# Keys loaded and turned before queries, and beta's product with the queries moved to TensorE, in the opening stage of a fused attention and mixture-of-experts kernel

## What is computed

```python
xn = layernorm(x)
# s: attention on xn
x_norm = layernorm(xn) * gamma + beta
q, k, v = x_norm @ qkv[:, :512], x_norm @ qkv[:, 512:1024], x_norm @ qkv[:, 1024:]
attn = softmax(causal(q @ k.T / sqrt(512)))
s = (attn @ v) @ o_proj + xn
# f: mixture of 8 experts (top 2 by the router) plus a shared expert
f = routed(xn, router_w, wg, wu, wd) + shared(xn, sg, su, sd)
out = x + s * silu(f)
```

## Time and profile before

| | |
|---|---|
| median of 3 runs | 1148.88 us (1148.87 to 1150.69) |
| profiled execution | 1149.01 us, of which 1147.2 us is the span of the trace |
| TensorE busy | 1130.9 us, 99% of the span |
| VectorE busy | 571.8 us, 50% |
| ScalarE busy | 473.0 us, 41% |
| granted TensorE clock, mean | 0.998 |

### The profile page before, as it was taken

One profiled execution on the slowest core, in us unless ns is written; L12 is line 12 of the kernel. 1 busy time (PEld: TensorE's weight loads), 2 busy tenths in 40 slices (PEclk: granted clock), 3 DMA queues, 4 the chain that ended last, 5 costly groups with the idle time before them and its releaser, 6 DMA issues. The chain is left out here.

```text
span 1147.2 us, 21220 instructions
## 1 busy us (share of the span) xinstructions
PE 1130.9 (99%) x6598; PEld 625.7 (55%) x6599; DVE 571.8 (50%) x1236; ACT 473.0 (41%) x859; POOL 420.3 (37%) x656
## 2 busy tenths in 40 slices
PE   8999999999999999999999999999999999999997
PEld 5555555555556555555555555554444444444443
DVE  7876667667469221221112211122477377367467
ACT  5544444344332223332223322234654545545643
POOL 1333233332400222222222222213755754764763
PEclk9999999999999999999999999999999999999999
DMA  9899999988533698998997877766876777766364
GB/s 283 241 227 214 229 245 222 226 206 243 127 78 74 126 202 198 204 204 203 206 193 189 179 182 179 181 163 155 166 183 172 166 160 189 157 160 183 107 161 116
DMA packets 365003, 209.31 MB, mean 182 GB/s; under 512 B 304308, under 2 KB 314816, under 8 KB 364936
## 3 DMA queue, kind: packets, MB, share of 16 engines
q1 hardware_dynamic: 354104, 172.76, 64.3%
q0 software_dynamic: 10800, 35.69, 12.1%
q10 hardware_dynamic: 32, 0.02, 0.0%
HBM read 89.44 MB, written 46.01 MB: 118 GB/s over the span
## 5 line engine op out<-in xcount | busy, mean ns | idle before, releaser
L706 PE MATMUL pair<-arena 128*128 (+2 forms) x3240 | 506.2, 313 | 0.3 <-issue 0.2
L706 PEld LDWEIGHTS pair<-arena 128*128 128x128 f16 x3240 | 315.7, 98 | 183.2 <-issue 1.5
L1646 DVE SCALAR_TENSOR_TENSOR arena<-pair,slot_unit,arena 128x352 f32<-128x352 f32 x71 | 41.4, 584 | 269.5 <-ACT arena L1536 269.5
L713 PE MATMUL bank<-arena 128*128 x639 | 149.4, 379 | 0.0
L1536 ACT ACTIVATE arena<-pair,slot_unit 128x352 f32<-128x352 f32 x71 | 39.3, 553 | 205.5 <-PE pair L706 202.4
L1251 POOL COPY arena<-token_of 128x1 uint32 (+1 forms) x71 | 12.9, 182 | 264.1 <-issue 107.0
L1942 PE MATMUL pair<-arena 128*128 128x512 f16 (+3 forms) x576 | 98.4, 326 | 1.1 <-ACT arena L2010 0.6
L713 PEld LDWEIGHTS bank<-arena 128*128 128x128 f16 x639 | 62.5, 98 | 66.3
L1955 PE MATMUL bank<-arena 128*128 128x512 f16 x411 | 93.6, 379 | 0.3 <-DVE arena L2122 0.3
L1253 POOL DMA_INDIRECT arena<-xn_rows,arena x71 | 71.4, 1006 | 55.6 <-POOL arena L1251 52.5
L1922 PE MATMUL bank<-arena 128*128 128x512 f16 x384 | 86.1, 379 | 0.0
(11 more groups left out here) (205 smaller groups left out, 1354.4 us busy)
## 6 DMA issues: line engine op xcount, KB each, us to landing
slot_rows<-arena SPq DMA_DIRECT2D x71, 256.0 KB
arena<-in_L_attn_x_dram SPq DMA_DIRECT2D x64, 256.0 KB, 3.4
xn_rows<-arena SPq DMA_DIRECT2D x32, 260.0 KB, 2.5
shared_rows<-arena SPq DMA_DIRECT2D x32, 256.0 KB, 3.4
arena<-shared_rows SPq DMA_DIRECT2D x32, 256.0 KB, 3.1
out_dram<-arena SPq DMA_DIRECT2D x31, 256.0 KB, 2.5
arena<-in_L_ffn_wg_dram SPq DMA_DIRECT2D x32, 176.0 KB, 3.0
arena<-in_L_ffn_wu_dram SPq DMA_DIRECT2D x32, 176.0 KB, 3.2
```

The costliest lines, as they stand in the source:

```text
L706: last = pe.matmul(bank[:, 0:width], xt[:, a, c, :], weights(c, b, col, width), start=(c == 0 and i == 0), stop=(c == KC - 1 and i == 2))
L713: last = pe.matmul(bank[:, :], ht[:, a, c, :], weights(c, b), start=(start and c == 0 and i == 0), stop=(stop and c == HC - 1 and i == 2))
L1646: v.scalar_tensor_tensor(sbuf[u], u_banks[u][:, 0:H], slot_unit[u][:, 1:2], sbuf[u], ALU.mult, ALU.mult).then_inc(slot_h_ready, 1)
```

## The change

The keys' two loads are issued ahead of the queries' four. The keys are turned first, into banks 0 to 3, with `turn_small` behind the second row block. The queries are then turned by row block: one bank takes the four transposes of one row block, so it holds all that one block of 128 output rows needs. Three query blocks are turned, then the first product is made (its 12 matmuls ordered by part instead of by chunk), then the fourth query block, then the other products. The products go to banks 0, 1, 2, 3, 6, 7, 4, 6. The order of high and low parts becomes keys, three query blocks, two value blocks, the fourth query block, two value blocks. `keep_small` and `split_small` come first on their engines. The load of repeated beta and the four `beta_row` are removed. Instead `query_beta`, behind the second product, makes 16 float32 matmuls of one column, and `split_ab` reads the result with one added instruction.

```diff
-            turns = [("turn", m, n) for m in range(2) for n in range(KC)]
+            k_turns = [("turn", 1, n) for n in range(KC)]
+            q_turns = [("turn", 0, k) for k in range(KC)]
+            v_parts = [("split_v", 2, k) for k in range(KC)]
             products = [("product", m, n) for m in range(2) for n in range(KC)]
-            on_pe = turns + products
+            on_pe = k_turns + q_turns[:3] + products[:1] + q_turns[3:] + products[1:]
+            first_groups = k_turns + q_turns[:3] + v_parts[:2] + q_turns[3:] + v_parts[2:]
+            groups = first_groups + products[:2] + [("split_o", 0, k) for k in range(KC)] + products[2:]
...
             def sync(sp):
                 q_rows = qkv.rearrange("(c p) n -> p c n", p=P)
-                for k in range(KC):
-                    sp.dma_start(w_qkv[:, k, 0:D], qkv[k * P:(k + 1) * P, 0:D]).then_inc(q_loaded[k], 16)
                 for i in range(2):
                     rows = slice(i * KC // 2, (i + 1) * KC // 2)
                     sp.dma_start(w_qkv[:, rows, D:2 * D], q_rows[:, rows, D:2 * D]).then_inc(k_loaded[i], 16)
+                for k in range(KC):
+                    sp.dma_start(w_qkv[:, k, 0:D], qkv[k * P:(k + 1) * P, 0:D]).then_inc(q_loaded[k], 16)
...
-                sp.dma_start(beta_rows, beta.partition_broadcast(P)).then_inc(beta_loaded, 16)
...
+                def turn_q(k):
+                    pe.wait_ge(q_loaded[k], 16)
+                    if k == KC - 1:
+                        pe.wait_ge(lo_done, made("turn", 0, 0))
+                    for n in range(KC):
+                        part = pe.transpose(banks[bank_of[("turn", 0, k)]][:, n * P:(n + 1) * P],
+                                            w_qkv[:, k, n * P:(n + 1) * P], ident)
+                    part.then_inc(group_done, 1)
...
+                def query_beta():
+                    pe.wait_ge(affine_kept, 4)
+                    for n in range(KC):
+                        for k in range(KC):
+                            last = pe.matmul(small[:, qb_at + n:qb_at + n + 1], w_qkv[:, k, n * P:(n + 1) * P],
+                                             affine[:, 1, k:k + 1], start=(k == 0), stop=(k == KC - 1))
+                    last.then_inc(ab_done, 1)
+
+                def first_product():
+                    bank = banks[bank_of[("product", 0, 0)]]
+                    for i, (a, b) in enumerate(PARTS):
+                        if i == 0:
+                            pe.wait_ge(hi_done, made("turn", 0, 0))
+                        else:
+                            pe.wait_ge(lo_done, made("turn", 1, KC - 1) if i == 1 else made("turn", 0, 0))
+                        for c in range(KC):
+                            if i == 0 and c == 0:
+                                pe.wait_ge(lo_done, made("turn", 1, 0))
+                            last = pe.matmul(bank[:, :], turned[:, 0, c, a, 0:P], turned[:, 1, c, b],
+                                             start=(c == 0 and i == 0), stop=(c == KC - 1 and i == 2))
+                    last.then_inc(group_done, 1)
...
-                for m in range(2):
-                    for k in range(KC):
-                        turn_row(m, k)
-                for n in range(KC):
+                for k in range(KC):
+                    turn_k(k)
+                    if k == 1:
+                        turn_small()
+                for k in range(3):
+                    turn_q(k)
+                first_product()
+                turn_q(KC - 1)
+                for n in range(1, KC):
                     product(0, n)
-                    if n == 0:
-                        turn_small()
+                    if n == 1:
+                        query_beta()
                 beta_products()
...
-                def beta_row(n):
-
-                    dve.wait_ge(beta_loaded, 16)
-                    wait(dve, ab_done, n)
-                    v.tensor_tensor_reduce(weighed, banks[n][:, :], beta_rows, S_AB, 0.0, ALU.mult, ALU.add,
-                                           accum_out=ab[:, 0, n:n + 1]).then_inc(ab_done, 1)
...
                 def split_ab():
-                    dve.wait_ge(ab_done, KC)
                     dve.wait_ge(uw_done, 1)
+                    dve.wait_ge(ab_done, 1)
+                    v.tensor_scalar(ab[:, 0, :], small[:, qb_at:qb_at + KC], S_AB, None, ALU.mult)
```

More of the change, by code:

```diff
@@ L356, in fold_programs @@
             bias_made = sem("bias_made")
-            turns = [("turn", m, n) for m in range(2) for n in range(KC)]
+            k_turns = [("turn", 1, n) for n in range(KC)]
+            q_turns = [("turn", 0, k) for k in range(KC)]
+            v_parts = [("split_v", 2, k) for k in range(KC)]
             products = [("product", m, n) for m in range(2) for n in range(KC)]
-            on_pe = turns + products
[L362 to L365, removed]
+            on_pe = k_turns + q_turns[:3] + products[:1] + q_turns[3:] + products[1:]
+            first_groups = k_turns + q_turns[:3] + v_parts[:2] + q_turns[3:] + v_parts[2:]
+            groups = first_groups + products[:2] + [("split_o", 0, k) for k in range(KC)] + products[2:]
+            bank_of = {**{g: n for n, g in enumerate(k_turns)}, **dict(zip(q_turns, (4, 6, 7, 4))),
+                       **dict(zip(products, (0, 1, 2, 3, 6, 7, 4, 6)))}
             def made(kind, m, n):
@@ L372, in group_target @@
                 kind, m, n = groups[g]
+                if kind == "turn" and m == 0:
+                    return turned[:, 0, :, :, n * P:(n + 1) * P].rearrange("p c s t -> p s c t"), S_QKVO
                 if kind == "turn":
-                    return turned[:, m, n], S_QKVO
+                    return turned[:, 1, n], S_QKVO
                 if kind == "split_v":
@@ L482, in product @@
                 def product(m, n):
-                    bank = banks[bank_of[on_pe.index(("product", m, n))]]
-                    q = m * KC + n
-                    if m == 1:
+                    bank = banks[bank_of[("product", m, n)]]
+                    if m == 0:
+                        pe.wait_ge(lo_done, made("turn", 0, n))
+                    else:
                         pe.wait_ge(v_moved[n // 2], 32)
-                    wait(pe, ab_done, rows_before[q])
-                    if q >= 5:
-                        pe.wait_ge(lo_done, made("product", 0, q - 5))
+                    if (m, n) == (1, KC - 1):
+                        pe.wait_ge(lo_done, made("product", 1, 0))
@@ L490, in product @@
                     for c in range(KC):
-                        if n == 0:
-                            pe.wait_ge(lo_done, made("turn", 1, c) if m == 0 else made("split_o", 0, c))
+                        if m == 1 and n == 0:
+                            pe.wait_ge(lo_done, made("split_o", 0, c))
                         for i, (a, b) in enumerate(PARTS):
@@ L543, in banks_free @@
             def banks_free(pe, b):
-                pe.wait_ge(lo_done, (made("product", 0, 3), made("product", 1, 0), made("product", 1, 3))[b])
-                if b < 2:
-                    pe.wait_ge(ab_done, b + 3)
+                pe.wait_ge(lo_done, (made("product", 0, 1), made("product", 0, 3), made("product", 1, 3))[b])
             def turn_bias(pe):
@@ L588, in keep_small @@
                                          ).then_inc(affine_kept, 1)
[L590 to L594, removed]
                 keep_small()
+                for g in first_groups:
+                    high(*g)
                 high("product", 0, 0)
@@ L661, in keep_bias @@
                                     ).then_inc(bias_made, 1)
[L663 to L669, removed]
+                split_small()
+                for g in first_groups:
+                    low(*g)
+                    if g == q_turns[2]:
+                        stats(dve, 0)
                 normalise(dve, 0)
                 low("product", 0, 0)
-                split_small()
-                beta_row(0)
-                beta_row(1)
                 low("product", 0, 1)
```

18 lines of the change are left out of this document (6 added, 12 removed).

## The result

The changed kernel is slower: 1154.88 us in the median of 9 executions (1150.72 to 1156.42) against 1149.19 (1147.76 to 1152.09), a ratio of 1.0043 with a 95% interval of 1.0032 to 1.0054, or 4.9 us. Two more measurements of the same file gave 1.0036 (1.0022 to 1.0049) and 1.0049 (1.0032 to 1.0066). The forecast was 1149.4 with a range up to 1152.2. The profiled execution of the changed kernel took 1156.42 us with a span of 1154.7, so it lies above its median, where that of before lay on it.

The account below looks back on a forecast made before the run. TensorE, busy 99% of the span, was taken as the bound: -1.33 - 0.10 - 0.40 + 0.47 + 3.1 = +1.8 us there, 1.3 absorbed by stalls, +0.5 at the end; 1149.4 us on the median, range 1147.8 to 1152.2.

Parts of the forecast that it names:

- First product at 10.8: Start of TensorE's first product in the fold, forecast at 10.8 us instead of 12.13: -1.33 us.
- rival of the late rate: TensorE's clock stays low through the first product: D = 4.6, the end +3.3 us, 1152.2; chance 0.10.
- Added products, 3.1 us: The 16 float32 matmuls of `query_beta` on TensorE, taken as three passes of 65 ns each: 3.1 us in all.
- Of TensorE's 1.8 us, 1.3 are absorbed by stalls: Up to the down product near 65 us, existing stalls take 1.3 us of the delay; +0.5 reaches the end.
- D: Delay of TensorE behind `query_beta`, forecast +1.8 us; from there up the end moves by about D - 1.3.
- the mark: Start of the shared expert's down product that waits for a DMA transpose: 64.96 us before, forecast 65.46.
- the copy at 46.69: ScalarE's copy in the chain to the stalled down product, forecast 0.5 us late, behind silu(1)'s work ending at 47.2.
- TensorE's few waits follow its own pace: After 65 us TensorE's waits were to move along with it.
- within 0.2%: Outcome that the end differs by less than 0.2% (2.3 us), which can't be told from none; chance 0.75.
- the case with 0.19: Outcome that the kernel is slower: long passes, late rate and rests; chance 0.19.
- the four passes: Rival: float32 products in `query_beta` take four passes, added 4.2 us, the end +1.6, 1150.5; chance 0.20.
- the gain: Rival: float32 matmuls of `query_beta` cost one pass (1.0 us), D = -0.3, the end -0.7, 1148.2; chance 0.12.

Follow-up runs that it names:

- after_warm: The changed kernel with 14 instead of 10 warm-up transposes and nothing else; ratio 1.0067 to the kernel before.
- new_order_ratio: The changed kernel without `query_beta`: the key side of `bias_folds` multiplies the finished fold by beta over gamma, in the same float16 matmuls; ratio 1.0005.
- after_beta_twice: The changed kernel with `query_beta` made twice in a row, 7.0 us of float32 products instead of 3.5; ratio 1.0113.
- before_filled: The kernel before with eight more idle transposes between the queries' and the keys' turns; ratio 1.0014.
- old_ratio_filled: old_order_ratio with the eight idle transposes of before_filled; ratio 1.0001.
- spread_warm: after_beta_spread with 14 instead of 10 warm-up transposes; ratio 1.0037.
- after_again: The changed kernel once more, nothing altered; ratio 1.0036.
- old_order_ratio: The kernel before without `beta_row` and the load of repeated beta, with beta over gamma times the finished fold in `bias_folds`; ratio 1.0001.
- after_beta_early: The changed kernel with 4 of the 16 products of `query_beta` put ahead of the first product; ratio 1.0050.
- after_beta_spread: The changed kernel with the 16 float32 products set one by one between the matmuls of products (0,1) to (0,3); ratio 1.0013.
- ratio_repeat16: new_order_ratio with 16 more float16 matmuls of 512 columns where the changed kernel has `query_beta`; ratio 1.0041.
- new_ratio_warm: new_order_ratio with 14 instead of 10 warm-up transposes; ratio 0.9976, and 0.9968 when run again.
- old_order_pe_beta: The kernel before with `beta_row` and its load removed and `query_beta` behind the third product, order and banks as before; ratio 1.0070.

## Why the prediction was wrong

The direction of TensorE's sum was right (later), the mechanism of VectorE was right (its freed time becomes a wait), and the end was forecast at +0.5 us where it is +4 to +5.6. The steps:

- **First product at 10.8.** It was 11.42, 11.25 and 11.40, so the start was worth 0.71 us and not 1.33 in the first profile. The keys landed at 4.9 instead of 4.8, which is nothing; the clock rose at 8.7 to 9.9 instead of about 7, so most key turns went at the half level. This is the rival of the late rate in its mild form. With the pause before the keys filled, and nothing else changed, it is 10.40 (after_warm; 10.42, 10.04 and 10.26 in the other three with 14 warm-up transposes), so this step is shown by experiment.
- **Added products, 3.1 us.** Measured 3.49 (109 ns for each of 32 pairs). The size was off by 0.4. The Trainium skill's page "FP8 and Floating Point Precision" (TensorE Precision Notes) gives four passes for true FP32, which with the 65 ns row was an estimate of 4.2 us. The trace shows two pairs of weight load and matmul for a product, 218 ns; whether such a pair is one pass or two the records don't tell.
- **"Of TensorE's 1.8 us, 1.3 are absorbed by stalls."** This is the step that failed. D, the delay of TensorE, was 2.7 and the mark moved by 2.17, so 0.5 us were absorbed up to there, and at the end nothing is left of that: the added 3.49 us raise the total by about 4.4 us (new_order_ratio against the changed kernel), 3.46 us of other work raise it by about 4.1. I followed the chain over the copy at 46.69 on ScalarE and gave that a slack of 1.15 us. There the reckoning held: the work behind silu(1) came 2.39 us late and the copy 1.31. But VectorE has its own queue there: the weight split at 45.02 stands behind `hidden` of unit 1 and behind ScalarE's part behind silu(1), so it waits for TensorE at once. It moved by 2.39 us, to 47.41. The only slack between it and the next splits was the 0.58 us of waiting at 48.30. Those splits moved by 1.73, and they took 3.38 us instead of 2.99. Why they took longer is not shown. A stall belongs to all chains that enter it, and the shortest slack counts. Experiment agrees: without `query_beta` (new_order_ratio) the mark moved back by 3.25 us of its 3.49. The slack of 0.58 us is read from the rows; no run changed it alone.
- **The clock behind `query_beta`.** Not foreseen. I priced the products by their length and looked for the clock only at its first rise. In six of the seven profiles with the float32 products in one stretch, the clock falls within the stretch or within 1.1 us behind it; in none of the eleven others does it fall between 15 and 60 us. At half the pace a fall of 3.4 us costs 1.7, one of 6.8 costs 3.4. The float16 one-column stretches of `bias_folds` (1.6 us) let no fall come.
- **After 65 us "TensorE's few waits follow its own pace".** Wrong too. From the mark to the end, 18 profiles take between 1080.2 and 1087.5 us. TensorE waits 0 to 3 us at the border to the attention stage (about 830 us), up to 1.7 at the first expert tiles (410 to 440 us), and up to 2.2 at single down products. The clock adds to it: in five profiles it fell for 3.4 us in or behind such a wait, of 2.1 to 3.1 us (at 76 us in after_beta_twice, 102 in before_filled, 827 to 832 in old_ratio_filled, spread_warm and after_again). These five take 1086.8 us on average from the mark on, the other thirteen 1083.8.

In sum, the forecast was +0.5 and the first measurement +4.9. In its profile the mark came at 67.13 where 65.46 was forecast: 1.0 us of that is the size of D, 0.7 the absorption. Averaged over the profiles the mark is at 68.75 in the changed kernel (67.13, 70.30, 68.81) and at 65.51 in the kernel before (64.96, 66.05), 3.2 us apart.

The mean clock on record gives the falls a size. Over a span of 1150 us, 0.9974 means 3.0 us of lost clock in the kernel before, and the 0.9968 of the 27 executions of the changed kernel means 3.7: by this estimate the clock is 0.7 us of the slowdown on average (0.4 and 1.6 us in the two measurements that have the clock of both kernels), and the length of the products most of it. An estimate of the total for each kernel is then what its order costs without beta work (0.6 us in the new order, from new_order_ratio, with an interval of 1.7 us to either side; 0.1 us in the old, from old_order_ratio), plus the added work, plus the clock lost beyond that of the kernel before (1150 us times the difference of the mean clocks):

| run | added work, us | lost clock, us | sum | measured |
|---|---|---|---|---|
| changed kernel (three measurements) | 3.5 | 0.7 | 4.8 | 4.1 to 5.6 |
| after_beta_twice | 7.0 | 6.0 | 13.6 | 13.0 |
| after_beta_early | 3.5 | 1.0 | 5.1 | 5.7 |
| after_beta_spread | 2.2 | -1.2 | 1.6 | 1.5 |
| ratio_repeat16 | 3.5 | -0.1 | 3.9 | 4.7 |
| after_warm | 3.5 | 1.4 | 5.5 | 7.7 |
| spread_warm | 2.2 | -0.8 | 2.0 | 4.3 |
| new_ratio_warm, and again | 0 | -0.8, -1.2 | -0.2, -0.6 | -2.8, -3.7 |
| old_order_pe_beta | 3.5 | 2.0 | 5.6 | 8.0 |
| old_ratio_filled | 0 | -1.0 | -0.9 | 0.1 |

In the new order with ten warm-up transposes the sums close within 0.8 us, with nothing absorbed. For the other kernels they miss by 1 to 3 us, to both sides, where the measured intervals reach 1.1 to 2.4 us to either side, and **that part stays open**. It is not the order: from the mark to the end the six profiles of the old order take 1084.5 us on average, the twelve of the new order 1084.7. So the gain of new_ratio_warm is measured twice but explained in part: it is 3.4 and 4.3 us faster than new_order_ratio, and its mark is 1.0 and 1.6 us earlier.

Of the chances: "within 0.2%" had 0.75, and it was the case with 0.19. (The forecast, the four passes and the gain, which the prediction counts as lying within 0.2%, add up to 0.77 already.) The range's upper end, 1152.2, came from a clock that stays low through the first product, which did not happen; the products at their full length, with nothing absorbed, are enough to go beyond it (1149.2 + 0.6 + 3.5 = 1153.3).

## What to carry to other kernels

Work moved from an engine with slack onto the one that is always busy costs its full length, and the freed engine turns its time into a wait; look for an algebraic form that needs no new work (here beta over gamma times the finished fold) before moving it. When a stall seems to absorb a delay, list every engine whose queue enters it and take the smallest slack. Price a stretch of tiny matmuls with the clock after it: in the two versions that spread them among full ones the same 16 products cost 2.2 us and no fall came, in one stretch they cost 3.5 us and the clock fell in six of seven profiles. The mean clock over all executions says what such falls cost on average, which one profile can't.

## What the runs showed of the hardware

- A float32 product of 128 by 128 weights and one column is two weight loads and two matmuls in the records, 109 ns a pair at the full level (3.49 us for 32) and about 214 ns at the half (the last 23 of 64 in 4.9 us); between full-column matmuls the whole product costs 140 ns.
- The clock can fall to its half level while TensorE is never idle, if what it runs are one-column float32 matmuls (it fell at 19.2 us in after_again, 2.3 us into the stretch, and at 21.5 in after_beta_twice, 4.5 us into it, and stayed there for 6.8 and 10.2 us). A stretch of 3.46 us of float16 matmuls with 512 columns in the same place let none come (ratio_repeat16, one profile).
- The clock's first rise came at 4.8 to 7.5 us where warm-up and turns follow each other closely, and at 8.7 to 11.5 us behind a pause of 0.7 to 1.1 us between warm-up and turns. Four more idle transposes (0.85 us) removed the pause and brought it back to 5.1 to 6.6 us in four profiles. The Trainium skill's page "TensorE: Matmul & The Clock Gate" (Part 4) says that transposes don't engage the full rate. The runs show otherwise: in all 18 profiles only transposes stood before the rise.
